# A layer of experts, attention and experts on one core: GpSimd's scatters reordered, one weighing moved to VectorE, and the table of row numbers requested by GpSimd

## The chip, the cores and the metric

One core of a Trainium2 chip runs the whole program in one launch. The metric is the device time of that launch in microseconds (us), the median over runs. Engines are named as the profile names them: PE is TensorE, DVE is VectorE, ACT is ScalarE, POOL is GpSimd, SP is SyncE. SP computes nothing here; it only issues DMA transfers in program order, and a wait in its program holds every transfer behind it.

## What is computed

Input `x` has 8 x 1024 rows of 256 numbers. The layer is a sandwich, cut here to what matters:

```python
def ffn(h):                       # 64 experts, the best 2 per row, 256 places per expert
    x = rmsnorm(h) * rms_w
    probs = softmax(x @ gate_w.T)
    w, ids = top_k(probs, 2); w = w / w.sum()
    buf[e, place] = x[row]        # rows are grouped by expert: this is the scatter
    y = (silu(buf @ w13[:, :I]) * (buf @ w13[:, I:])) @ w2      # per expert
    moe[row] = sum over the 2 chosen experts of w * y[e, place] # and back
    shared = silu(x @ sw_gate) * (x @ sw_up) @ sw_down
    return moe + shared + h

x = x + 0.5 * ffn(layernorm(x))
x = x + attention(layernorm(x))   # three MLPs and a masked, softmax-free attention
x = x + 0.5 * ffn(layernorm(x))   # same weights again: "the second experts"
```

The change is at the passage from the attention to the second `ffn`.

## The kernel before

The attention works on 16 groups of 512 rows, which the code calls halves of a sequence (`HALVES = 16`, `j` or `h` counts them; `last` is 15). While TensorE does the matrix products of group `j`, the other engines finish group `j - 2`: they normalise its rows for the second `ffn`, ask TensorE for the router's logits, choose two experts per row, count how many earlier rows chose the same expert, and so give each row its two slots in DRAM. GpSimd then writes each row to its two slots: `scatter_rows` (L1182) issues 8 indirect DMAs per group into `slot_rows`, 128 rows each. `scatter_meta` (L1197) issues 8 more into `slot_ids`: for each slot the number of the row that sits in it, 4 bytes each.

After the last group nothing of the attention is left to hide this work, so the two last groups (14 and 15) form a chain, here called the passage. For group 15 it runs:

- VectorE `out_statistics` writes `attention_o_under`;
- GpSimd `out_roots` (L1166) takes the power -1/2 (`routing_affine`);
- VectorE `out_scales` (L1521) makes the scale and shift;
- ScalarE `normalise` (L1306) writes the rows, four tiles of 128x256, into `xn_last`, which lies in `attention_t_rows`; each tile raises `normed`;
- `weigh` (L1170) multiplies them by the row `rms_w`, on GpSimd, one instruction for all four tiles;
- TensorE `turn_x` (L1961) transposes them, ScalarE copies them (`attention_w_rows`), TensorE `router` (L1969) makes the logits, VectorE `choose` and `mark` pick the experts, GpSimd `counts` (L1174), TensorE `place_tiles`, VectorE `places` and `slots` give the addresses;
- GpSimd `scatter_rows(15)` issues the 8 row scatters.

GpSimd issues in the order in which its code is written, and between the steps of group 15 it scatters the rows and row numbers of group 14.

The 64 experts follow. SP loads an expert's 256 slots (`load_slots`, L1067, into a ring of `YR` = 4 buffers) and its weights (`load_w13`, `load_w2`, rings of 8; the first eight are loaded long before). Expert `e` goes: TensorE `turn_slots(e)` (L2116), ScalarE and VectorE split the rows and weights in two parts, TensorE `gate_up(e)` (L2129), ScalarE's silu, TensorE `expert_down(e)` (L2139), ScalarE `copy_y(e)` (L1399) into a ring of 4, and GpSimd two indirect DMAs (L1280) that write the 256 results back by row number into `token_rows`. These need the table `who` (`attention_gelu` in the traces), which is `slot_ids` read back. SP loads it: after `load_slots` 0 to 3 its program waits for all row-number scatters, issues the table and only then goes on with `load_slots(4)` and the weights of expert 8. Three waits bind the loop: `load_slots(e)` waits for `turn_slots(e - 4)`; `load_w2(e)` waits for `expert_down(e - 8)`; `copy_y(e)` waits until the scatters of expert `e - 4` have landed.

## Time and profile before

| | us |
|---|---|
| median of 3 runs | 2216.04 |
| lowest and highest of them | 2206.85, 2218.53 |
| the profiled execution | 2217.58 |
| its span, from first to last instruction | 2215.4 |
| share of the span in which PE is busy | 89% |

The profiled execution is the one that the rows come from; it took 2.2 us more than its span and 1.5 us more than the median. Times of rows are us from the start of its span. The passage lies at 1829 to 1874, the experts at 1874 to about 2084, the shared part and the sum behind them.

### The profile page before, as it was taken

The numbers are of one execution on the slowest core, as the hardware profiler recorded it, in microseconds if no ns is written. First come the engines' busy times: TensorE is split into PE (matmuls) and PEld (weight loads), VectorE is DVE, ScalarE is ACT, GpSimd is POOL, SyncE is SP. The second block draws the span as 40 slices with busy tenths as digits, with TensorE's granted clock in tenths as the row PEclk, the third lists the DMA queues.
The fourth block names the chain that finished last, engine by engine and source line by source line (L and its number), as shares of the span: only waits on it lengthen the run. The fifth ranks groups of instructions, "written<-read, shape, count | busy, mean of one in ns | idle before, by whom it ended". The sixth has DMA issues, their size and how long they took to land.

```text
span 2215.4 us, 32427 instructions
## 1 busy us (share of the span) xinstructions
PE 1978.3 (89%) x11044; PEld 1675.5 (76%) x11044; DVE 1324.0 (60%) x3515; ACT 1085.1 (49%) x1988; POOL 1105.9 (50%) x1202
## 2 busy tenths in 40 slices
PE   6886888779999999999999999999999972888887
PEld 4665788658888888888888878878888862887754
DVE  6996555355576566576576575565565442554467
ACT  6774666434454454454454354444453442555643
POOL 5665666453245545545545645645525316555500
PEclk9998999989999999999999999999999985999999
DMA  8433888792032021121121210110100202888778
GB/s 274 144 105 129 269 272 275 245 301 61 1 96 67 30 95 38 59 95 41 56 89 31 73 43 21 52 39 20 58 10 20 86 10 67 274 274 287 240 250 280
DMA packets 236405, 270.06 MB, mean 122 GB/s; under 512 B 25489, under 2 KB 186322, under 8 KB 236242
## 3 DMA queue, kind: packets, MB, share of 16 engines
q1 hardware_dynamic: 199122, 192.40, 27.7%
q0 software_dynamic: 28672, 67.22, 9.3%
q10 hardware_dynamic: 8448, 8.39, 1.1%
q8 instruction: 88, 1.44, 0.3%
q14 instruction: 75, 0.61, 0.1%
HBM read 150.35 MB, written 117.57 MB: 121 GB/s over the span
## 4 chain that ended last, share of the span: by engine, by line
PE 60%; DVE 8%; issue 5%; ACT 4%; POOL 1%; DMA 1%; another core or an unknown queue 1%; SPq 0%; ACTq 0%; DVEq 0%; POOLq 0%
PE attention_ring L1926 20%; PE attention_acc L1956 13%; PE attention_acc L1946 8%; DVE attention_hid_l L1659 2%; PE attention_work L2016 2%; PE attention_work L1999 2%; PE attention_work L2032 2%; PE attention_work L2036 2%; PE attention_acc L2139 2%; PE attention_ring L2129 2%; PE attention_ring L2165 2%; PE attention_acc L2129 1%; PE attention_work L1914 1%; PE attention_ring L2116 1%; PE attention_work L1973 1%
## 5 line engine op out<-in xcount | busy, mean ns | idle before, releaser
L1659 DVE TENSOR_TENSOR attention_hid_l<-attention_gelu,attention_hid_h 128x512 fp32r<-128x512 f32 x384 | 284.5, 741 | 504.4 <-ACT attention_gelu L1303 320.3
L1300 ACT ACTIVATE attention_hid_h<-attention_ring,home_b 128x512 fp32r<-128x512 f32 x384 | 264.2, 688 | 572.6 <-PE attention_ring L1926 500.0
L1303 ACT ACTIVATE attention_gelu<-attention_ring,home_b 128x512 f32<-128x512 f32 x384 | 261.7, 682 | 0.0
L1956 PE MATMUL attention_acc<-attention_hid_h,home_w_h 128*128 128x512 f32 x512 | 203.9, 398 | 21.0 <-DVE home_room L1685 18.7
L1926 PE MATMUL attention_ring<-attention_n_t_h,home_w_h 128*128 128x512 f32 x512 | 206.0, 402 | 1.4 <-DVE attention_n_t_l L1651 1.4
L1926 PE MATMUL attention_ring<-attention_n_t_l,home_w_h 128*128 128x512 f32 x512 | 201.7, 394 | 0.0
L1926 PE MATMUL attention_ring<-attention_n_t_h,home_w_l 128*128 128x512 f32 x512 | 201.6, 394 | 0.0
L1956 PE MATMUL attention_acc<-attention_hid_l,home_w_h 128*128 128x512 f32 x512 | 200.3, 391 | 0.0
L1956 PE MATMUL attention_acc<-attention_hid_h,home_w_l 128*128 128x512 f32 x512 | 200.2, 391 | 0.0
L1147 POOL DMA_INDIRECT home_room<-expert_rows,routing_slots x128 | 135.9, 1061 | 98.3 <-issue 53.8
L648 POOL DMA_INDIRECT experts_xg<-xn_rows,routing_affine x128 | 141.8, 1108 | 71.9 <-PE experts_ps_t L741 35.3
L1280 POOL DMA_INDIRECT token_rows<-home_room,attention_gelu x128 | 127.8, 999 | 97.6 <-ACT home_room L1399 53.0
L1192 POOL DMA_INDIRECT slot_rows<-attention_xn,attention_slot_at x120 | 123.3, 1027 | 95.5 <-DVE attention_meta_at L1595 63.6
L1946 PE MATMUL attention_acc<-home_w_h,attention_hid_h 128*128 128x256 f32 x512 | 145.2, 284 | 0.4 <-issue 0.4
L1203 POOL DMA_INDIRECT slot_ids<-attention_row_id,attention_meta_at x128 | 127.1, 993 | 36.6 <-issue 36.5
L1946 PE MATMUL attention_acc<-home_w_h,attention_hid_l 128*128 128x256 f32 x512 | 144.8, 283 | 0.0
L1946 PE MATMUL attention_acc<-home_w_l,attention_hid_h 128*128 128x256 f32 x512 | 144.5, 282 | 0.0
L1956 PEld LDWEIGHTS attention_acc<-attention_hid_h,home_w_h 128*128 128x128 f32 x512 | 96.9, 189 | 52.2 <-DVE home_room L1685 24.2
L1926 PE MATMUL attention_ring<-attention_m_t_h,home_w_h 128*128 128x512 f32 x256 | 112.3, 439 | 1.4 <-DVE attention_m_t_l L1651 1.4
L1926 PEld LDWEIGHTS attention_ring<-attention_n_t_l,home_w_h 128*128 128x128 f32 x512 | 97.1, 190 | 21.3
L1956 PEld LDWEIGHTS attention_acc<-attention_hid_l,home_w_h 128*128 128x128 f32 x512 | 96.6, 189 | 20.8
L1926 PEld LDWEIGHTS attention_ring<-attention_n_t_h,home_w_h 128*128 128x128 f32 x512 | 97.3, 190 | 19.4 <-DVE attention_n_t_l L1651 1.8
(277 smaller groups left out, 5247.1 us busy)
## 6 DMA issues: line engine op xcount, KB each, us to landing
experts_w<-in_L_ffn_w SPq DMA_DIRECT2D x64, 256.0 KB
expert_rows<-experts_y SPq DMA_DIRECT2D x64, 256.0 KB
slot_rows<-const_zeros SPq DMA_DIRECT2D x16, 1024.0 KB
token_rows<-const_zeros SPq DMA_DIRECT2D x16, 1024.0 KB
home_room<-in_L_ffn_w SPq DMA_DIRECT2D x64, 256.0 KB
home_room<-slot_rows SPq DMA_DIRECT2D x64, 256.0 KB
final_y_rows<-token_rows SPq DMA_DIRECT2D x32, 512.0 KB, 7.4
dispatch_x_in<-in_L_attn_x SPq DMA_DIRECT2D x16, 512.0 KB, 7.1
```

The lines of the kernel that those rows point to most:

```text
L648: pool.indirect_dma_start(out=xg[e % R][:, c, :], out_offset=None, in_=xn_d, in_offset=bass.IndirectOffsetOnAxis(ap=routing["lists"][:, e, ...
L1147: pool.indirect_dma_start(out=ye[:, t, k, :], out_offset=None, in_=y_d, in_offset=bass.IndirectOffsetOnAxis(ap=routing["slots"][:, j * GT ...
L1192: pool.indirect_dma_start(out=xs_d, out_offset=bass.IndirectOffsetOnAxis(ap=slot_at[h % 2][:, k, t:t + 1], axis=0), in_=xn_of(h)[:, t, :], ...
L1203: pool.indirect_dma_start(out=meta_d, out_offset=bass.IndirectOffsetOnAxis(ap=meta_at[h % 2][:, k, t:t + 1], axis=0), in_=row_id[h % 2][:, ...
L1280: pool.indirect_dma_start(out=y2_d, out_offset=bass.IndirectOffsetOnAxis(ap=who[:, e, c:c + 1], axis=0), in_=y[e % YR][:, c, :], in_offset ...
L1300: act.activation(hid[n % PARTS][0][:, :], ring[n % RING][:, :], ACT.Gelu, bias=b1[:, m, c:c + 1])
L1303: act.activation(gelu[n % GELUS][:, :], ring[n % RING][:, :], ACT.Gelu, bias=b1[:, m, c:c + 1]).then_inc(ring_free, 1)
L1659: dve.tensor_tensor(hid[n % PARTS][1][:, :], gelu[n % GELUS][:, :], hid[n % PARTS][0][:, :].bitcast(fp32), ALU.subtract).then_inc(hid_read ...
L1926: last = pe.matmul(ring[n % RING][:, :], w1[m][wp][:, k, c * P:(c + 1) * P], rows_t[xp][:, k, :], start=(q == 0), stop=(q == 2 * len(TERMS ...
L1946: last = pe.matmul(acc[e % 3][:, (t % 2) * D:(t % 2 + 1) * D], hid[s][xp][:, t * P:(t + 1) * P], w2[m][wp][:, c, :], start=(c == 0 and q = ...
L1956: last = pe.matmul(acc[e % 3][:, :], w2[m][wp][:, c, k * P:(k + 1) * P], hid[s][xp][:, :], start=(c == 0 and q == 0), stop=(c == FC - 1 an ...
L2129: last = pe.matmul(ps_gu[e % EF][:, half, :], wt[e % EF][:, k, half * INNER:(half + 1) * INNER], xt[e % EF][:, k, :], start=(n == 0), stop ...
```

## The change

Four edits, all at the passage. (1) GpSimd's `out_roots(15)` comes after 4 instead of 6 of group 14's row scatters; the other 4 follow it, and the row-number scatters of group 14 are split 4, 3 and 1 instead of 5 and 3, the one left over being issued behind the rows of group 15. (2) The weighing of group 15 leaves GpSimd: VectorE does it tile by tile, four instructions, each after the tile's `normed`. A new semaphore `last_weighed` tells of it, and TensorE's `turn_x` and GpSimd's row scatters of group 15 wait for that. VectorE's second split of weights, `split_weights(1)`, now stands behind the weighing. (3) SP no longer waits for the row-number scatters nor loads the table. (4) GpSimd waits for them itself and requests the table, behind its last row-number scatter and ahead of the experts' result scatters.

```diff
@@ sync
             sp.wait_ge(y2_zeroed, 16 * FILLS)
-            for h in (HALVES - 2, HALVES - 1):
-                sp.wait_ge(*scattered(meta_scattered, h))
-            sp.dma_start(who, meta_d[0:SLOTS, :].rearrange("(p e c) a -> p e (c a)", p=P, c=CH)).then_inc(who_loaded, 16)
@@ gpsimd, scatter_rows
                 pool.wait_ge(slots_ready, 4 * (h + 1))
-                pool.wait_ge(weighed, h + 1)
+                if h < HALVES - 1:
+                    pool.wait_ge(weighed, h + 1)
+                else:
+                    pool.wait_ge(last_weighed, GT)
@@ gpsimd
             counts(last - 1)
-            scatter_rows(last - 1, 0, 6)
+            scatter_rows(last - 1, 0, 4)
             out_roots(last)
-            scatter_rows(last - 1, 6, 8)
-            weigh(last)
-            scatter_meta(last - 1, 0, 5)
+            scatter_rows(last - 1, 4, 8)
+            scatter_meta(last - 1, 0, 4)
             counts(last)
-            scatter_meta(last - 1, 5, 8)
+            scatter_meta(last - 1, 4, 7)
             scatter_rows(last)
+            scatter_meta(last - 1, 7, 8)
             scatter_meta(last)
-
+            for h in (last - 1, last):
+                pool.wait_ge(*scattered(meta_scattered, h))
+            pool.dma_start(who, meta_d[0:SLOTS, :].rearrange("(p e c) a -> p e (c a)", p=P, c=CH)).then_inc(who_loaded, 16)
             pool.wait_ge(who_loaded, 16)
@@ vector
             out_scales(last)
             split_weights(0)
+            for t in range(GT):
+                dve.wait_ge(normed, GT * last + t + 1)
+                dve.tensor_tensor(xn_of(last)[:, t, :], xn_of(last)[:, t, :], rms_w[:, :], ALU.mult).then_inc(last_weighed, 1)
             split_weights(1)
@@ tensor, turn_x
-                pe.wait_ge(weighed, j - 1)
+                if j <= HALVES:
+                    pe.wait_ge(weighed, j - 1)
+                else:
+                    pe.wait_ge(last_weighed, GT)
```

On GpSimd, from the row scatters of group 14 to the end of the passage, the order before was as follows (`slot_rows` are row scatters, `slot_ids` row-number scatters; `attention_xn` holds group 14, `attention_t_rows` group 15):

```order
L1192 DMA slot_rows<-attention_xn,attention_slot_at 32768x256 x6
L1168 TENSOR_TENSOR routing_affine<-attention_o_under,const_minus_half 128x2x4
L1192 DMA slot_rows<-attention_xn,attention_slot_at 32768x256 x2
L1172 TENSOR_TENSOR attention_t_rows<-attention_t_rows,routing_rms_w 128x1024
L1203 DMA slot_ids<-attention_row_id,attention_meta_at 32768x1 x5
L1182 TENSOR_TENSOR attention_before<-attention_carry,attention_either 128x64
L1182 TENSOR_TENSOR attention_before<-attention_before,attention_either 128x64 x2
L1182 TENSOR_TENSOR attention_carry<-attention_before,attention_either 128x64
L1203 DMA slot_ids<-attention_row_id,attention_meta_at 32768x1 x3
L1192 DMA slot_rows<-attention_t_rows,attention_slot_at 32768x256 x8
L1203 DMA slot_ids<-attention_row_id,attention_meta_at 32768x1 x8
```

And the same stretch in the changed kernel:

```order
L1193 DMA slot_rows<-attention_xn,attention_slot_at 32768x256 x4
L1166 TENSOR_TENSOR routing_affine<-attention_o_under,const_minus_half 128x2x4
L1193 DMA slot_rows<-attention_xn,attention_slot_at 32768x256 x4
L1204 DMA slot_ids<-attention_row_id,attention_meta_at 32768x1 x4
L1180 TENSOR_TENSOR attention_before<-attention_carry,attention_either 128x64
L1180 TENSOR_TENSOR attention_before<-attention_before,attention_either 128x64 x2
L1180 TENSOR_TENSOR attention_carry<-attention_before,attention_either 128x64
L1204 DMA slot_ids<-attention_row_id,attention_meta_at 32768x1 x3
L1193 DMA slot_rows<-attention_t_rows,attention_slot_at 32768x256 x8
L1204 DMA slot_ids<-attention_row_id,attention_meta_at 32768x1 x9
L1278 DMA attention_gelu<-slot_ids 128x128
```

The roots moved two scatters forward, the weighing (`routing_rms_w`) is gone, one row-number scatter went behind the rows of group 15, and the table's load is new at the end.

On VectorE, at the point where `out_scales(15)` has run, the changed kernel has this (`attention_n_t_l` is the split of an expert's weights; before, its two instructions stood together and the weighing was absent):

```order
L1532 SCALAR_TENSOR_TENSOR routing_affine<-attention_o_mv,routing_affine 128x4
L1808 TENSOR_TENSOR attention_n_t_l<-home_room,attention_n_t_h 128x512
L1848 TENSOR_TENSOR attention_t_rows<-attention_t_rows,routing_rms_w 128x256 x4
L1808 TENSOR_TENSOR attention_n_t_l<-home_room,attention_n_t_h 128x512
L1540 MAX attention_top<-attention_work 128x8 x4
```

The four weighings stand between the two splits, ahead of the search for the best experts.

On SP, before, from the two last stores of the attention's rows on (`home_room<-slot_rows` is an expert's slots, `home_room<-in_L_ffn_w` weights):

```order
L1041 DMA base_rows<-home_room 128x4x256 x2
L1070 DMA home_room<-slot_rows 128x512 x4
L1097 DMA attention_gelu<-slot_ids 128x128
L1070 DMA home_room<-slot_rows 128x512
L1059 DMA home_room<-in_L_ffn_w 128x512
```

And now:

```order
L1042 DMA base_rows<-home_room 128x4x256 x2
L1071 DMA home_room<-slot_rows 128x512 x5
L1060 DMA home_room<-in_L_ffn_w 128x512
```

The table's load no longer stands between the fourth and the fifth expert's slots.

## Rows read from the trace of the kernel before

**Rows 1.** The page's busy time of each engine and its share.

```profile
PE 1978.3 (89%) x11044; PEld 1675.5 (76%) x11044; DVE 1324.0 (60%) x3515; ACT 1085.1 (49%) x1988; POOL 1105.9 (50%) x1202
```

**Rows 2.** Busy time by stretch: stretch, length, engines, PEclk, DMA share, GB/s.

```profile
1829.00:1841.00 12.00, 0.26 (x3) 0.06 (x1) 4.46 (x17) 2.08 (x4) 10.15 (x9) 0.64 0.22 77
...
1890.00:1904.00 14.00, 12.45 (x88) 11.71 (x87) 9.05 (x21) 7.42 (x16) 9.63 (x10) 1.00 0.93 312
1904.00:1910.00 6.00, 5.58 (x41) 5.18 (x40) 3.82 (x7) 4.03 (x9) 2.36 (x3) 1.00 0.64 184
1910.00:2050.00 140.00, 122.16 (x825) 114.20 (x824) 70.02 (x123) 78.64 (x164) 83.52 (x83) 0.96 0.87 282
2050.00:2080.00 30.00, 27.44 (x191) 25.32 (x190) 15.45 (x28) 22.35 (x50) 17.17 (x19) 1.00 0.98 318
```

**Rows 3.** Timeline of GpSimd at the roots and the weighing: start, duration.

```profile
1833.39 0.96 POOL L1192 DMA_INDIRECT slot_rows<-attention_xn,attention_slot_at  x1 [0.30 <-issue]
1834.38 1.68 POOL L1168 TENSOR_TENSOR routing_affine<-attention_o_under,const_minus_half 128x8 f32<-128x8 f32 x1
1836.24 1.04 POOL L1192 DMA_INDIRECT slot_rows<-attention_xn,attention_slot_at  x1 [0.19 <-issue]
1837.58 0.96 POOL L1192 DMA_INDIRECT slot_rows<-attention_xn,attention_slot_at  x1 [0.30 <-issue]
1838.63 2.33 POOL L1172 TENSOR_TENSOR attention_t_rows<-attention_t_rows,routing_rms_w 128x1024 f32<-128x1024 f32 x1
```

**Rows 4.** Timeline of VectorE, ScalarE and TensorE in the same stretch.

```profile
1831.82 0.16 DVE L1519 TENSOR_SCALAR attention_o_under<-attention_o_mv 128x4 f32<-128x4 f32 x1
...
1836.36 1.28 DVE L1805 TENSOR_TENSOR attention_n_t_l<-home_room,attention_n_t_h 128x512 fp32r<-128x512 f32 x2
1836.47 2.08 ACT L1313 ACTIVATE attention_t_rows<-home_room,routing_affine 128x256 f32<-128x256 f32 x4 [9.17 <-DVE routing_affine L1529]
...
1841.02 1.33 PE L1966 MATMUL attention_work<-const_eye,attention_t_rows 128*128 128x128 f32 x5 [11.76 <-POOL attention_t_rows L1172]
```

**Rows 5.** Timeline of VectorE, a product of two 128x256 tiles.

```profile
1882.21 0.42 DVE L1817 TENSOR_TENSOR attention_state<-attention_state,attention_acc 128x256 f32<-128x256 f32 x1
```

**Rows 6.** Timeline of GpSimd from the counts to the first result scatter.

```profile
1850.15 0.30 POOL L1182 TENSOR_TENSOR attention_before<-attention_carry,attention_either 128x64 bf16<-128x64 bf16 x1 [2.96 <-DVE attention_either L1555]
...
1851.76 0.99 POOL L1203 DMA_INDIRECT slot_ids<-attention_row_id,attention_meta_at  x1 [0.15 <-issue]
...
1855.58 0.96 POOL L1192 DMA_INDIRECT slot_rows<-attention_t_rows,attention_slot_at  x1 [0.30 <-DVE attention_meta_at L1595]
...
1864.44 0.96 POOL L1192 DMA_INDIRECT slot_rows<-attention_t_rows,attention_slot_at  x1 [0.31 <-issue]
...
1874.56 0.96 POOL L1203 DMA_INDIRECT slot_ids<-attention_row_id,attention_meta_at  x1 [0.31 <-issue]
1886.74 0.96 POOL L1280 DMA_INDIRECT token_rows<-home_room,attention_gelu  x1 [11.22 <-DMA attention_gelu<-slot_ids]
```

**Rows 7.** Timeline of SP's queue at the end of the passage.

```profile
1866.94 1.76 SPq L1070 DMA_DIRECT2D home_room<-slot_rows  x4
1882.73 0.32 SPq L1097 DMA_DIRECT2D attention_gelu<-slot_ids  x1
1883.10 1.02 SPq L1070 DMA_DIRECT2D home_room<-slot_rows  x1
```

**Rows 8.** Timeline of TensorE, its two waits for slots.

```profile
1873.93 1.96 PE L2116 MATMUL attention_ring<-const_eye,home_room 128*128 128x128 f32 x8 [21.66 <-DMA home_room<-slot_rows]
...
1887.34 0.74 PE L2116 MATMUL attention_ring<-const_eye,home_room 128*128 128x128 f32 x4 [1.95 <-DMA home_room<-slot_rows]
```

**Rows 9.** Timeline of ScalarE, copies of the first and fifth expert's results.

```profile
1884.14 0.59 ACT L1399 ACTIVATE home_room<-attention_acc 128x512 f32<-128x512 f32 x1
...
1897.44 0.59 ACT L1399 ACTIVATE home_room<-attention_acc 128x512 f32<-128x512 f32 x1
```

**Rows 10.** DMA issues, 1850 to 1890: KB, us from issue to landing.

```profile
attention_gelu<-slot_ids SPq DMA_DIRECT2D x1, 64.0 KB, 3.7
```

More of the change, by code:

```diff
@@ L1003, in attention_to_end @@
         odds_ready, f_step, f_scaled, halved = sem("odds_ready", late=True), sem("f_step", late=True), sem("f_scaled", late=True), sem("halved", late=True)
+        last_weighed = sem("last_weighed", late=True)
         f_normed, f_turned, xf_t_ready, sw_weighed = sem("f_normed"), sem("f_turned"), sem("xf_t_ready"), sem("sw_weighed")
```

## The prediction

> **What bounds the kernel now.** The page's busy times come first: TensorE is busy for 89% of the span and no other engine for more than 60% [rows 1]. Over the whole kernel the rule is therefore that only what TensorE waits for counts, and the change touches about 60 us of 2215. So the next view is the table by stretches, then the timeline of each engine through the passage. In 1829 to 1841 TensorE works 0.26 of 12 us [rows 2]: it stands idle for 11.76 us until the weighing on GpSimd is done at 1838.63 + 2.33 = 1840.96 [rows 3, 4]. It works briefly on the logits and is then idle for 21.66 us until the first expert's slots have landed, at 1873.93 [rows 8]. What ends last there is GpSimd's queue and the transfers behind it: the eight row scatters of group 15 start at 1855.58 and the last at 1864.44, SP issues the slot loads at 1866.94, and the first lands 7.0 us later [rows 6, 7, 8]. Behind that, SP stands: its last slot load of four is out at 1868.7, and the next transfer, the table, goes at 1882.73, with the fifth expert's slots at 1883.10 [rows 7]. TensorE waits 1.95 us for these slots, at 1887.34 [rows 8]. From 1910 on the experts run with TensorE busy for 122.16 of 140 us and the DMA engines at 0.87 [rows 2]: neither is full.
>
> **Edit 1, the roots two scatters earlier.** VectorE has their input at 1831.82 + 0.16 = 1831.98, GpSimd starts them at 1834.38, right behind the sixth scatter, which began at 1833.39 [rows 3, 4]. A scatter takes its 0.96 plus 0.30 of issue, 1.27 from start to start: four instead of six end at 1834.35 - 2 x 1.27 = 1831.8, just ahead of the input. From an input to GpSimd's start I take 0.08, the step from ScalarE's last tile (1836.47 + 2.08 = 1838.55) to the weighing at 1838.63 [rows 3, 4]. New start 1832.06, gain 2.32. The chain behind (roots 1.68, VectorE's scales, four tiles on ScalarE) keeps its lengths: tiles done at 1836.23.
>
> **Edit 2, the weighing on VectorE.** On GpSimd it is one instruction that waits for all four tiles and takes 2.33 [rows 3]. On VectorE only the last tile's quarter is left after ScalarE's last tile. The trace of before has no 128x256 product of these two operands; the nearest row is 0.42 for two 128x256 tiles [rows 5], the bounds are 0.42 / 2 (were it to run at twice that rate) and 0.64 (the 128x512 split, 1.28 for two [rows 4]). I take 0.42, plus 0.04 for the hand-over: TensorE can start at 1836.23 + 0.04 + 0.42 + 0.06 = 1836.75 instead of 1841.02. Edits 1 and 2 together gain 4.27, of which edit 2 is 1.95. The first three weighings lie beside ScalarE's tiles (2.08 for four, 0.52 each) and cost nothing. `split_weights(0)` lies ahead of the tiles, `split_weights(1)` behind them; the second is first needed by the second expert, 35 us later. VectorE has nothing else until the logits, so the cover is wide.
>
> GpSimd must not become late in its turn. Roots end at 1833.74, eight scatters (four of rows, four of row numbers) begin at 1833.92 and at 1.27 each, with the 1.34 of the first as in [rows 3], end by 1843.8. The counts may start 4.27 earlier than now, at 1845.9 [rows 6]: 2.0 us of slack. Counts and three row-number scatters, as before, give 1851.3 for the first row scatter of group 15, where it was 1855.58. Before, its addresses and the third row-number scatter were ready within a tenth of a us of each other, so neither hides the gain. The row-number scatter put behind costs only the table 1.27. Slots are then issued by SP at 1866.94 - 4.27 = 1862.7 and expert 0 starts at 1869.7.
>
> A lock between the two engines is a rule that speaks against this edit. The row first: VectorE's two splits ran at 1836.36 for 1.28, beside a row scatter on GpSimd from 1836.24 that took 1.04 instead of 0.96 [rows 3, 4], so 0.08 is all that the pair lost, and the sum stays as it is. The Trainium skill (SBUF — State Buffer, "Who interferes with whom") says that a VectorE instruction with two inputs in SBUF contends with a GpSimd instruction that reads SBUF, and the one that comes second waits for the other's end. Taken by that rule with scatters as readers, the last weighing would begin up to a scatter's length later, and the sum would be about 1 us less; that is the rival "lock" below.
>
> The clock gives nothing back. TensorE is idle for 11.76 us, and the granted clock over 1829 to 1841 is 0.64 [rows 2, 4]: of 12 us some 3.4 at the full 2.4 GHz and the rest at 1.2, so it fell near 1832.4, ahead of 1836.75. The transposes and the router will still run at half clock.
>
> **Edits 3 and 4, the table.** SP may issue the fifth expert's slots when `turn_slots(0)` is done, about 1.0 into the pair at 1873.93, thus at 1875.0 in the old times and 1870.7 in the new; before it was 1883.10, 8.1 later. Loads of slots took 7.0 (1866.94 to 1873.93) and 4.2 (1883.10 to 1887.34) [rows 7, 8]. Even with 7.0 they are there at 1877.7, and TensorE wants them at 1887.34 - 1.95 - 4.27 = 1881.1: the wait of 1.95 goes whole. The loads that SP sent in one burst from 1883 on made DMA engines 0.93 busy in 1890 to 1904, and TensorE was idle for 1.55 there and 0.42 in 1904 to 1910 [rows 2]; spread out, they cost between 0 and 2.0. I take half, 1.0.
>
> The table now goes later by the moved scatter and by GpSimd's own issue. Row numbers: first at 1851.3 + 8 x 1.27 = 1861.4, the ninth begins at 1871.6 and ends at 1872.5. Before, from the last one's end (1874.56 + 0.96 = 1875.52) to SP's issue 7.2 passed; I keep that, since its cause is not in the rows: 1879.7. Landing: SP's took 3.7 [rows 10], and 4.0 to the first result scatter [rows 6, 7]. No row has a plain load issued by GpSimd; its scatters need 0.96 before their bytes go, SP's issue 0.32. Between 3.7 and 7.0 + 1 I take 4.3: result scatters start at 1884.0. The Trainium skill (DMA: Bandwidth & Descriptors, "Specifications") gives about 1 us to the first byte for a DMA that GpSimd issues against about 0.6 for one of SP's; by it the sum for the table would be 0.4 more than SP's, near what I take. Who waits: ScalarE's copy of the fifth result, which needs the first expert's two scatters landed. It stood at 1897.44 [rows 9], now 1897.44 - 7.2 = 1890.2. Two scatters from S are landed at S + 1.27 + 2.5 (the last row scatter of the passage took 2.5 from start to SP's release, 1864.44 to 1866.94). So S may be as late as 1886.4; 1884.0 leaves 2.4. Hidden, but with a thin cover.
>
> **Sum.** 4.27 + 1.95 + 1.0 = 7.2 us. Against the profiled execution's 2217.58 that is 2210.4 (span 2208.2). That execution lies 1.5 above the median, so for the median 2216.04 - 7.2 = 2208.8. All behind expert 5 is a loop of waits among engines and rings, with no fixed date in it, so I let a shift pass through whole.
>
> **Rivals.** In times of the profiled execution; take 1.5 off for the median.
> - Only the head start arrives (chance 0.25). Either the table is later than 1886.4, or the DMA engines bind: 0.87 at 282 GB/s for 140 us and 0.98 at 318 in 2050 to 2080 [rows 2] speak for it; against it speaks that the 0.87 leaves an eighth of their time free. The stage begins 4.27 earlier and keeps just that: 2213.3.
> - More than forecast (0.12). The loads run ahead by all of SP's idle stretch, 7.2 from the last row number to the table, and TensorE's waits in 1910 to 2050 shrink too: 4.27 + 7.2 = 11.5, 2206.1. Against it: the rings are short, and SP is soon back at the pace of `expert_down`.
> - The lock (0.08): 6.2, 2211.4. The 0.08 in the rows is against it; the rule of the Trainium skill above is for it.
> - The change does not act at the roots or the place search (0.05): something else, as the addresses, holds GpSimd; gain 3, 2214.6.
> - Slower (0.05): the table becomes the bound. It used to be loaded while nothing else moved; now slots and weights are in flight. Slots needed 7.0 instead of 4.2 beside the small scatters. If wait and load of the table took twice 11.5, S would be 1872.5 + 23 = 1895.5, and the fifth copy, with the next silu and the next rows' split behind it on ScalarE, and so TensorE, would be 9.1 late: +1.9, 2219.5. It decides from S = 1893.6 on.
>
> The forecast has 0.45.
>
> **How the numbers follow.** About 0.5% (11 us) is what a measurement of this kernel tells from no change. The median forecast is 2208.8. Cases from 11.5 gained to 1.9 lost give medians 2204.5 to 2218; the runs of before alone lie 11.7 apart, so I widen a little to 2201 to 2219. Faster by over 0.5% means under 2205: half of the third case, the edge of the forecast and the runs' scatter give 0.16. Slower by over 0.5% needs 18 us of new waits: 0.03. The rest, 0.81, is within.
>
> **What will show it.** GpSimd's roots at 1832.1; the last of four VectorE weighings ending near 1836.7, each about 0.42; TensorE's transposes after 7.5 idle instead of 11.76; the first row scatter of group 15 at 1851.3; slots issued at 1862.7; the fifth slots issued within 1871 and no wait of TensorE for them; the table issued near 1880 and result scatters from 1884. I would be wrong if the addresses came later than 1851.3, if the fifth copy waited for landed scatters, or if TensorE's idle time in the later experts grew by what the start had saved.

## The result and the profile after

| | us |
|---|---|
| before, median of 20 runs | 2212.78 (2199.78 to 2226.75) |
| changed, median of 20 runs | 2222.46 (2214.09 to 2231.74) |
| ratio, with its 95% interval | 1.0049 [1.0035, 1.0063] |
| changed, profiled execution; its span | 2224.62; 2222.7 |

The change costs 10.8 us by the ratio, 7.7 to 13.9 by its interval; 7.2 saved were forecast. The profiled execution had reached the passage 7.13 us sooner than the one of before, by chance, so below the places are compared by their distance from one instruction, the first row scatter of group 14 on GpSimd: 1826.65 before, 1819.52 after. I call it "offset".

The page's busy line has hardly moved against [rows 1]; only TensorE has 9 us more, with the same number of instructions:

```profile
PE 1987.3 (89%) x11044; PEld 1683.2 (76%) x11044; DVE 1323.8 (60%) x3519; ACT 1085.2 (49%) x1988; POOL 1103.6 (50%) x1202
```

The table by stretches, at the places of [rows 2] moved by 7 us (stretch, length, engines, PEclk, DMA share, GB/s):

```profile
1822.00:1834.00 12.00, 3.82 (x18) 3.29 (x17) 6.05 (x21) 5.05 (x10) 9.44 (x10) 0.68 0.22 77
1883.00:1897.00 14.00, 10.77 (x70) 9.84 (x69) 6.36 (x15) 4.36 (x9) 8.73 (x9) 0.95 0.61 203
1897.00:1903.00 6.00, 3.10 (x13) 3.06 (x14) 1.71 (x3) 1.99 (x4) 2.88 (x3) 0.58 0.42 157
1903.00:2043.00 140.00, 120.56 (x782) 111.74 (x781) 67.50 (x119) 76.03 (x160) 78.11 (x78) 0.92 0.82 269
```

In the first stretch TensorE works 3.82 us where it had 0.26: the head start is there. In the next two it works 13.9 of 20 us where it had 18.0, and in the first of them the DMA engines move 203 GB/s where they moved 312. The granted clock (PEclk) is 0.95, 0.58 and 0.92 in the last three stretches, where it was 1.00, 1.00 and 0.96. The start of the experts is where the gain is lost. From the first copy of an expert's result to the ninth, before and then in the changed kernel:

```profile
1884.14:1912.36 28.22, 24.30 (x168) 22.27 (x166) 15.82 (x33) 15.20 (x33) 15.40 (x16) 1.00 0.87 278
1871.36:1910.25 38.89, 28.51 (x169) 26.05 (x167) 16.16 (x33) 15.55 (x33) 16.06 (x17) 0.82 0.71 191
```

Of the 10.7 us by which this stretch is longer, 6.5 are idle time of TensorE and 4.2 are busy time: nearly the same matmuls at a mean granted clock of 0.82 in place of 1.00.

The timelines of VectorE, ScalarE and TensorE answer to [rows 4]:

```profile
1824.68 0.16 DVE L1522 TENSOR_SCALAR attention_o_under<-attention_o_mv 128x4 f32<-128x4 f32 x1
1827.03 2.08 ACT L1316 ACTIVATE attention_t_rows<-home_room,routing_affine 128x256 f32<-128x256 f32 x4 [6.85 <-DVE routing_affine L1532]
1827.66 1.91 DVE L1848 TENSOR_TENSOR attention_t_rows<-attention_t_rows,routing_rms_w 128x256 f32<-128x256 f32 x4
1829.62 1.97 PE L1975 MATMUL attention_work<-const_eye,attention_t_rows 128*128 128x128 f32 x8 [7.49 <-DVE attention_t_rows L1848]
```

TensorE's transposes stand at offset 10.10, before at 1841.02 - 1826.65 = 14.37: the 4.27 of the forecast to the hundredth, and the idle time of 7.49 too. GpSimd's timeline answers to [rows 3] and [rows 6]:

```profile
1824.93 1.67 POOL L1166 TENSOR_TENSOR routing_affine<-attention_o_under,const_minus_half 128x8 f32<-128x8 f32 x1 [0.23 <-issue]
...
1829.41 0.99 POOL L1193 DMA_INDIRECT slot_rows<-attention_xn,attention_slot_at  x1 [0.31 <-issue]
...
1844.18 0.96 POOL L1193 DMA_INDIRECT slot_rows<-attention_t_rows,attention_slot_at  x1 [0.30 <-DVE attention_meta_at L1598]
...
1864.44 0.96 POOL L1204 DMA_INDIRECT slot_ids<-attention_row_id,attention_meta_at  x1 [0.30 <-issue]
1879.82 0.60 POOL L1278 DMA_DIRECT2D attention_gelu<-slot_ids  x1 [14.42 <-DMA slot_ids<-attention_row_id,attention_meta_at]
1885.70 1.01 POOL L1283 DMA_INDIRECT token_rows<-home_room,attention_gelu  x1 [5.28 <-DMA attention_gelu<-slot_ids]
```

The first row scatter of group 15 is 4.27 earlier too, and expert 0 starts even 5.4 earlier (offset 41.87 against 47.28), since its slots took 5.8 us and not 7.0. But the wait between the last row-number scatter and the table has doubled, 14.42 us in place of 7.2, and the first result scatter starts 5.88 behind the start of the table's issue, where it was 4.01. Result scatters start at offset 66.18, before at 60.09. SP's queue, against [rows 7]:

```profile
1855.56 7.33 SPq L1071 DMA_DIRECT2D home_room<-slot_rows  x5
1862.93 0.44 SPq L1060 DMA_DIRECT2D home_room<-in_L_ffn_w  x1
1869.87 0.33 SPq L1065 DMA_DIRECT2D home_room<-in_L_ffn_w  x1
1870.24 0.43 SPq L1071 DMA_DIRECT2D home_room<-slot_rows  x1
```

SP no longer stands: five slot loads, the weights of expert 8 and the sixth slot load are out while, before, the table was still being waited for. TensorE's waits for slots, against [rows 8], and ScalarE's copies of the fifth and the ninth result, against [rows 9]:

```profile
1861.39 1.95 PE L2125 MATMUL attention_ring<-const_eye,home_room 128*128 128x128 f32 x8 [20.52 <-DMA home_room<-slot_rows]
...
1879.62 1.13 PE L2125 MATMUL attention_ring<-const_eye,home_room 128*128 128x128 f32 x4 [4.25 <-DMA home_room<-slot_rows]
...
1890.59 0.60 ACT L1402 ACTIVATE home_room<-attention_acc 128x512 f32<-128x512 f32 x1 [1.46 <-DMA token_rows<-home_room,attention_gelu]
...
1910.25 0.59 ACT L1402 ACTIVATE home_room<-attention_acc 128x512 f32<-128x512 f32 x1
```

The wait of 1.95 for the fifth expert's slots is gone. The one at 1879.62 is for the sixth's, requested at 1870.24 and 9.4 us on the way. The granted clock falls during this wait and again in a later idle stretch of 5.16 us that ends at 1899.90; behind each, TensorE works for nearly 5 us at half clock:

```profile
1879.60:1884.20 4.60, 4.58 (x19) 4.40 (x20) 1.71 (x3) 1.99 (x4) 0.60 (x1) 0.50 0.77 268
1899.90:1904.70 4.80, 4.80 (x18) 4.33 (x19) 1.42 (x3) 2.01 (x5) 1.82 (x2) 0.50 0.25 87
```

The fifth copy then waits for scatters that have not landed. The ninth copy stands at offset 90.7, before at 85.7. Last, the transfers themselves, in 40 equal slices (busy tenths, GB/s), first the changed kernel from 1861 to 1885:

```profile
DMA  9991502344010135299951499296996459999510
GB/s 397 406 199 15 94 14 17 75 65 31 27 14 27 51 48 75 65 336 366 253 20 7 38 104 41 73 32 85 145 99 58 53 207 353 386 410 418 184 41 0
```

and the kernel before, from 1867 to 1883:

```profile
DMA  0094900041304238999940000000000000040000
GB/s 1 0 77 92 92 0 0 5 113 51 20 26 36 67 51 338 395 390 410 330 132 6 1 1 0 0 0 0 0 0 0 0 0 0 0 20 0 0 0 0
```

Between 1863 and 1880 the changed kernel moves mostly 15 to 100 GB/s, but for a burst near 1872, with engines that often count as busy, though five loads and more are under way. It is back at 400 just as the wait of 14.42 ends. Before, the loads of four experts crept likewise for 5 us and then ran at 330 to 410; after that nothing moved for 6 us, and the table was requested into the quiet.

### The profile page after: what moved, and what is told of

Read it like the earlier page. It is cut to its first block, busy times and chain, and to the rows that moved or that the text cites. A ratio compares the mean times of both kernels' runs of the same rounds, so it can differ in the third digit from the quotient of the medians.

```text
span 2222.7 us, 32431 instructions
## 1 busy us (share of the span) xinstructions
PE 1987.3 (89%) x11044; PEld 1683.2 (76%) x11044; DVE 1323.8 (60%) x3519; ACT 1085.2 (49%) x1988; POOL 1103.6 (50%) x1202
## 4 chain that ended last, share of the span: by engine, by line
PE 59%; DVE 8%; issue 7%; ACT 4%; DMA 1%; another core or an unknown queue 1%; POOL 1%; SPq 0%; ACTq 0%; DVEq 0%; POOLq 0%
PE attention_ring L1932 19%; PE attention_acc L1962 13%; PE attention_acc L1952 7%; DVE attention_hid_l L1662 2%; PE attention_work L2025 2%; PE attention_work L2008 2%; PE attention_work L2041 2%; PE attention_work L2045 2%; PE attention_acc L2148 2%; PE attention_ring L2138 2%; PE attention_ring L2174 2%; PE attention_work L1920 1%; PE attention_acc L2138 1%; DMA home_room<-slot_rows 1%
## 5 line engine op out<-in xcount | busy, mean ns | idle before, releaser
L648 POOL DMA_INDIRECT experts_xg<-xn_rows,routing_affine x128 | 141.9, 1109 | 72.2 <-PE experts_ps_t L741 35.2
```

The source lines that it names most:

```text
L648: pool.indirect_dma_start(out=xg[e % R][:, c, :], out_offset=None, in_=xn_d, in_offset=bass.IndirectOffsetOnAxis(ap=routing["lists"][:, e, ...
```

## The theories

**Contention.** Loads let go while GpSimd's row-number scatters are being written creep, and hold up the completion of the scatters. SP's old wait for the table had kept the two apart. The harm comes from edit 3.

**Late table.** The harm comes from GpSimd requesting the table (edit 4): wait, issue and landing are longer, result scatters queue, copies wait.

**Head start lost.** Edits 1 and 2 themselves give nothing or cost, in a stage of experts that has another bound. This can hold beside either of the others.

The runs fell on four chips beside that of the result (chip A); the kernel before takes 2194.07 on B, 2152.95 on C, 2151.67 on D and 2194.54 on E. Ratios are against it on the same chip. Offsets are of the profiled execution. "Wait" is from the end of the last row-number scatter to the table's issue; in g2 four slot loads go first, and 7.4 is the time to the first of them (9.3 to the table). The kernel before has traces on A and D alone, so on B, C and E offsets are compared across chips; the changed kernel did not run on C and D.

| kernel, chip | ratio, 95% interval | wait | first result scatter | ninth copy |
|---|---|---|---|---|
| before, A | | 7.2 | 60.1 | 85.7 |
| b0 before, D | | 8.7 | 60.2 | 84.0 |
| changed, A | 1.0049 [1.0035, 1.0063] | 14.4 | 66.2 | 90.7 |
| e0 changed, B | 1.0029 [1.0014, 1.0044] | 12.7 | 64.3 | 90.2 |
| e0 changed, E | 1.0032 [1.0017, 1.0047] | 15.5 | 66.8 | 91.5 |
| e1 edits 1 and 2, B | 0.9997 [0.9983, 1.0012] | 7.5 | 56.7 | 81.1 |
| e1 edits 1 and 2, C | 0.9998 [0.9988, 1.0007] | 7.3 | 57.0 | 81.0 |
| e2 edits 3 and 4, B | 1.0023 [1.0008, 1.0037] | 10.2 | 63.4 | 86.9 |
| e2 edits 3 and 4, E | 1.0017 [0.9997, 1.0038] | 8.8 | 61.8 | 85.2 |
| e3 changed, loads held, B | 1.0005 [0.999, 1.0019] | 8.7 | 59.6 | 86.4 |
| f3 one load ahead, C | 0.9992 [0.9981, 1.0003] | 9.2 | 59.2 | 81.4 |
| v2 the same, table by SP, D | 0.9997 [0.9984, 1.0011] | 8.1 | 56.6 | 81.8 |
| f1 no row numbers of group 15, C | 0.9963 [0.995, 0.9976] | 3.5 | 52.8 | 74.6 |
| g2 nothing beside the scatters, E | 1.0053 [1.0036, 1.0069] | 7.4 | 69.1 | 94.5 |

## Experiments: which edit costs

**e1_passage_only.** Edits 1 and 2 alone. Against the changed kernel:

```diff
@@ sync
             sp.wait_ge(y2_zeroed, 16 * FILLS)
+            for h in (HALVES - 2, HALVES - 1):
+                sp.wait_ge(*scattered(meta_scattered, h))
+            sp.dma_start(who, ...).then_inc(who_loaded, 16)
@@ gpsimd
-            for h in (last - 1, last):
-                pool.wait_ge(*scattered(meta_scattered, h))
-            pool.dma_start(who, ...).then_inc(who_loaded, 16)
```

> The first two edits alone: GpSimd's new order with half of the weighing on VectorE; the table of row numbers is loaded by SyncE, ahead of the second experts' slot loads, as before the change. Contention theory (slot loads let go while the row-number scatters are still being written slow those scatters and crawl themselves): SyncE's wait for the table keeps them apart, so the table is requested about 7.2 us behind the last row-number scatter, result scatters begin about 12.8 us behind expert 0's first up product as before, and 4 to 6 us are gained: ratio 0.997 to 0.998. Late-table theory (the harm is that GpSimd issues the table, with a longer wait and landing): the same gain. If instead the first two edits cost time in the later experts, the ratio is 1.00 or above.

Measured: 2191.21 against 2194.07, ratio 0.9997 [0.9983, 1.0012]. The wait and the order of the start came as expected, the gain did not: no difference can be told from zero, and a gain of more than 3.7 us is excluded. Both theories of the table had expected 4 to 6 us; "head start lost" is borne out as far as the time goes.

**e2_table_only.** Edits 3 and 4 alone, in the kernel before: SP's three lines out, GpSimd's three in behind `scatter_meta(last)`.

> The last two edits alone: the table of row numbers is requested by GpSimd behind all counts, and SyncE no longer waits for it; GpSimd's order and the weighing are as before the change. Both theories expect it slower than before: the wait for the table about 14 us in place of 7.2, the fifth expert's slot load 9 us in place of 4 to 7, 9 to 14 us lost, ratio 1.004 to 1.006. If the loss came from the first two edits, it would be 0.998 to 1.001.

Measured: 2197.7, ratio 1.0023 [1.0008, 1.0037]. Slower beyond the interval, though by half of what was expected; the wait was 10.2, not 14.

**e3_hold_loads.** The changed kernel with SP's wait put back, and GpSimd still requesting the table:

```diff
@@ sync
             sp.wait_ge(y2_zeroed, 16 * FILLS)
+            for h in (HALVES - 2, HALVES - 1):
+                sp.wait_ge(*scattered(meta_scattered, h))
```

> The changed kernel with one thing put back: SyncE waits for both halves of the row-number scatters before the slot loads of the fifth expert and those behind it; GpSimd still requests the table. Contention theory: the wait for the table falls from 14.4 to about 7 us, the fifth slot load takes 4 to 7 us, ratio 0.997 to 0.998 as with the first two edits alone. Late-table theory: the table stays late since GpSimd issues it (landing near 5.6 us, results behind it), ratio 1.002 to 1.005.

**e0_after_again.** The changed kernel itself.

> The changed kernel unchanged, on the same chip as the three others, as the measure for them. All theories: ratio near 1.005, and the table waited for about 14 us.

Measured on the one chip: e3 2195.1, ratio 1.0005 [0.999, 1.0019]; the changed kernel 2199.5, ratio 1.0029 [1.0014, 1.0044]. With two lines of waiting no loss against the kernel before can be told. The gain that the contention theory had expected on top (0.997 to 0.998) did not come. GpSimd's timeline in the changed kernel and then in e3:

```profile
1860.53 0.59 POOL L1278 DMA_DIRECT2D attention_gelu<-slot_ids  x1 [12.65 <-DMA slot_ids<-attention_row_id,attention_meta_at]
1866.40 1.00 POOL L1283 DMA_INDIRECT token_rows<-home_room,attention_gelu  x1 [5.28 <-DMA attention_gelu<-slot_ids]
```

```profile
1858.30 0.59 POOL L1280 DMA_DIRECT2D attention_gelu<-slot_ids  x1 [8.72 <-issue]
1863.32 1.00 POOL L1285 DMA_INDIRECT token_rows<-home_room,attention_gelu  x1 [4.43 <-DMA attention_gelu<-slot_ids]
```

The wait falls from 12.65 to 8.72 with the loads held, as contention has it. The late table is left with what e3 has and e1 has not: GpSimd as the one that requests it. That costs the first result scatter 2.9 us (59.6 against 56.7), and 0.0008 in the ratio, less than either interval. The times of chip B alone do not divide the loss: e3's median of 2195.1 lies about halfway between e1's 2191.21 and the changed kernel's 2199.5, and the intervals of neighbours touch. That edit 4 costs little rests on f3 below, which has it too and runs at 0.9992 [0.9981, 1.0003] on chip C. So edit 3 is what costs, shown by the waits and likely by the times; edit 4 costs little if anything.

**e1_again.** Edits 1 and 2 once more.

> The first two edits alone once more, to narrow its interval. If the 4.27 us that the trace shows at expert 0 reach the end, the ratio is 0.998; if the later stretch is paced by transfers that start again only 2.8 us earlier, 0.9985 to 0.9995; if they are lost altogether, 1.000.

Measured on chip C: 2152.3 against 2152.95, ratio 0.9998 [0.9988, 1.0007]. A gain of 0.4 us, at most 2.6: the 4.27 of the passage doesn't reach the end whole. TensorE's wait for the slots of the fifth expert, and the stretch behind it:

```profile
1840.95 1.13 PE L2125 MATMUL attention_ring<-const_eye,home_room 128*128 128x128 f32 x4 [3.23 <-DMA home_room<-slot_rows]
```

```profile
1840.90:1844.10 3.20, 3.15 (x15) 3.15 (x16) 1.29 (x2) 1.60 (x3) 1.65 (x3) 0.50 1.06 395
```

Expert 0 starts some 6 us earlier than in b0 (offset 41.71 against 47.83), but SP issues the fifth slots only 4.4 earlier (53.51 against 57.88). So TensorE's wait for them is 3.23 where b0 has 1.27 and the trace of before on chip A 1.95, and behind it TensorE runs 3.2 us at half clock where b0 stays at 1.00. By the sixth copy 2.9 us of lead are left.

**e0_third, e2_third.** The changed kernel, and edits 3 and 4 alone, on chip E.

> The changed kernel on this chip, to see whether its loss is the same where the experts' stretch is paced by TensorE as much as by transfers. All theories of the passage: table waited for 10 us and more, sixth output copy at 77 to 80 us against 74 to 75 of before, ratio 1.002 to 1.005. If the loss was only of chips with slower transfers, 1.000 or below.

> The last two edits alone on this chip. Contention theory: the slot loads of the first four experts come when the row-number scatters are nearly done (5 us later than in the changed kernel), so the wait is 10 us and not 12 to 14, and the loss about half of the changed kernel's: ratio 1.001 to 1.003, less than e0_third's by 0.001 and more although it lacks the head start of the first two edits.

Measured: 1.0032 [1.0017, 1.0047] and 1.0017 [0.9997, 1.0038], with waits of 15.5 and 8.8. On both chips on which both ran, edits 3 and 4 alone cost less than with the head start of 1 and 2 on top, as contention predicts: the head start brings the loads nearer to the beginning of the row-number scatters. The intervals overlap, on B almost wholly, so the times don't show this order; of the mechanism it is the waits that speak.

## Experiments: what crawls, and what of it is contention

**f1_no_last_ids.** The changed kernel without `scatter_meta(last)`, the eight row-number scatters of group 15; the table waits for group 14's row numbers only. What it leaves out is the return of group 15's results to their rows.

> The changed kernel without the eight row-number scatters of the last group (that part is left out: the results of its tokens go to the spare row); the table waits only for the group before. Contention theory: nothing small is being written when SyncE lets the loads go, so the second experts' first five slot loads and weights 8 come at 200 GB/s and more, the fifth slot load takes 4 to 5 us and not 9, nothing waits for the table, and the time falls by 8 to 14 us against before: ratio 0.994 to 0.997. Late-table theory: the table comes early too, but the loads stay as slow as in the changed kernel (fifth slot load 9 us): ratio 0.997 to 0.999.

Measured: 2144.91 against 2152.95, ratio 0.9963 [0.995, 0.9976]. GpSimd's timeline and SP's:

```profile
1824.37 0.96 POOL L1204 DMA_INDIRECT slot_ids<-attention_row_id,attention_meta_at  x1 [0.30 <-issue]
1828.82 0.59 POOL L1276 DMA_DIRECT2D attention_gelu<-slot_ids  x1 [3.49 <-DMA slot_ids<-attention_row_id,attention_meta_at]
```

```profile
1825.60 7.06 SPq L1071 DMA_DIRECT2D home_room<-slot_rows  x5
1832.71 0.43 SPq L1060 DMA_DIRECT2D home_room<-in_L_ffn_w  x1
```

and the transfers from 1825.6 to 1849.6, slices as above:

```profile
DMA  0698092499944398000000000969849699987999
GB/s 1 72 82 10 0 113 34 157 403 393 410 184 24 130 376 345 0 0 0 0 0 14 0 0 12 234 157 369 314 85 260 109 420 389 324 208 239 381 415 348
```

The same loads are let go at the same place as in the changed kernel. Without the eight small scatters beside them the fifth slot load and expert 8's weights come at 345 to 376 GB/s, TensorE has no second wait for slots, and the ninth copy is at 74.6, where the changed kernel has 90 to 91. The first 4 us of the first four slot loads creep here as well, at 10 to 113 GB/s; the one row-number scatter and the rows that are still being written may be the reason, or the slow start may be the loads' own.

**g2_no_loads_beside.** The other way round, on top of e1: even `load_slots(0)` to `(3)` wait until all row numbers are written, so nothing is loaded beside them.

> The first two edits, with SyncE holding back even the first four slot loads until both halves of the row-number scatters are written, so that nothing at all is transferred beside them; table by SyncE. Contention theory: the wait behind the last row-number scatter falls from 7.3 to 8.7 us to about 3.5 us, as in the kernel without the last group's scatters. If 7 to 8 us are the scatters' own time to completion, it stays there. Expert 0 then starts 7 to 14 us later than in e1, so slower: ratio 1.002 to 1.004.

Measured: 2204.66 against 2194.54, ratio 1.0053 [1.0036, 1.0069]. GpSimd's last row-number scatter and SP's first load:

```profile
1850.86 0.95 POOL L1209 DMA_INDIRECT slot_ids<-attention_row_id,attention_meta_at  x1 [0.30 <-issue]
```

```profile
1859.22 1.76 SPq L1071 DMA_DIRECT2D home_room<-slot_rows  x4
1861.09 0.36 SPq L1100 DMA_DIRECT2D attention_gelu<-slot_ids  x1
```

That is 1859.22 - 1851.81 = 7.4 us with nothing beside. The 3.5 that I expected of the contention theory was wrong: the 7.2 of the kernel before is the scatters' own time, and the first four slot loads don't lengthen it measurably. Behind one such scatter 3.5 us pass (f1), behind nine in a row 7.4. They are issued every 1.27 us; an estimate from the two, if each of the nine takes alike, is 1.27 + (7.4 - 3.5) / 8 = 1.8 us for each to be written, so they pile up. The Trainium skill (DMA: Bandwidth & Descriptors, "Specifications") says that transfers under 512 bytes are done by reading, changing and writing back. These have 4 bytes, and a slow completion would fit; no run here had wider row numbers, so that cause is not shown.

**f3_hold_after_fifth.** The changed kernel with SP's wait behind `load_slots(4)`, one load later than in e3.

```diff
@@ sync
             for e in range(YR, EXPERTS):
                 load_slots(e)
+                if e == YR:
+                    for h in (HALVES - 2, HALVES - 1):
+                        sp.wait_ge(*scattered(meta_scattered, h))
```

> The changed kernel, where SyncE waits for both halves of the row-number scatters one load later than in e3: behind the slot load of the fifth expert, ahead of weights 8. If the crawl comes from the sum of the loads (three more of 128 to 256 KB), one load more is nearly free: wait for the table 8 to 10 us behind the last row-number scatter, ratio as e3, 1.000. If any load beside the row-number scatters delays them, the wait is 12 us and more and the ratio 1.002 to 1.003.

**v2_fifth_then_table.** The same, but SP requests the table, right behind that wait.

> The first two edits; SyncE requests the fifth slot load as soon as its buffer is free, then waits for both halves of the row-number scatters, requests the table itself, ahead of weights 8 and all behind. One load beside the row-number scatters is to cost them at most 2 us (9.20 in f3 against 7.5), the table comes ahead of the loads and lands 1 us sooner than in f3. Contention theory: ratio 0.998 to 0.9995. If the order of table and loads means nothing, the ratio of f3, 0.9992, or above.

Measured: f3 2152.67, ratio 0.9992 [0.9981, 1.0003]; v2 2152.16, ratio 0.9997 [0.9984, 1.0011]. One load beside the scatters is nearly free: waits of 9.2 and 8.1 against 7.2 to 8.7 with the first four slot loads alone. The three or more that the changed kernel lets go make it 12.7 to 15.5. So the size of the overlap matters, not that there is one. f3 falls within its expectation; v2's ratio is the one expected if the order of table and loads means nothing, though its result scatters start 2.7 us sooner. Neither can be told from the kernel before. In both, TensorE now waits for the sixth expert's slots, 3.9 and 4.4 us.

## Experiments: where the head start goes

**f7_weights_early.** On top of e1, `load_w13(8)` and `load_w13(9)` are issued ahead of SP's wait for the last rows and left out of the loop.

> The first two edits alone, as e1, and two loads of weights (w13 of experts 8 and 9, 256 KB each) requested ahead of SyncE's wait for the last rows, where the transfer queues are 0.2 busy, in place of among the second experts' loads. If the stretch of the second experts is paced by its transfers (0.86 busy at 280 GB/s in e1), 0.5 MB less in it is worth 0.5/0.28 = 1.9 us, and e1's own head start adds: ratio 0.997 to 0.999. If the stretch is paced by TensorE, or the early loads delay the row scatters, the ratio is that of e1, 0.9997, or above.

Measured: 2151.84, ratio 0.9998 [0.9987, 1.0008], the ninth copy at 81.8: no gain over e1 (0.9998, 81.0) can be told. The 1.9 us that were expected if transfers pace the stretch lie inside the interval, so this run decides little.

**b0_before_again, f5_less_tensor_work, f6_less_loads**, all on chip D; f5 and f6 are the kernel before with one edit each. f5 leaves out one of three terms of a product and is less exact; f6 leaves out the loads of down weights from the ninth expert on and takes those of the first eight, so its results are not the layer's:

```diff
@@ f5: gate_up of the second experts
-                terms = ((w13_hi, x_hi), (w13_lo, x_hi), (w13_hi, x_lo))
+                terms = ((w13_hi, x_hi), (w13_lo, x_hi))
@@ f6: load_w2; expert_down waits for the first load of its buffer only
                 if e >= WR:
-                    sp.wait_ge(y_ready, e - WR + 1)
+                    return
```

> The kernel before once more, for its trace on this chip. All theories: first output copy 57.5 us behind the first row scatter of group 14, the sixth 73 to 74, table requested 7.2 us behind the last row-number scatter. If TensorE has no waits in the stretch of the experts 6 to 43, it takes 107 us (as e1 on one chip); if it waits for weights, 122 to 129.

> The kernel before, where the second experts' gate and up products leave out one of their three terms (hidden values are less exact): four of some sixteen matmul pieces, 1.2 us of TensorE for each of 64 experts, 77 us in all. If the stretch is paced by its transfers (0.86 to 0.97 busy), the time falls by 0 to 15 us, ratio 0.993 to 1.000; if by TensorE, by 50 us and more, ratio under 0.977.

> The kernel before, where the second experts from the ninth on load no down weights (they use those of the first eight; results differ): 128 of 896 KB for each of 56 experts. If the stretch is paced by its transfers, 0.4 us for each, 25 us in all, ratio 0.988; where TensorE has no waits in it, at most 5 us, ratio 0.998 to 1.000.

Measured: f5 2139.17 against 2151.67, ratio 0.9944 [0.9927, 0.996]; f6 2141.7, ratio 0.9946 [0.9931, 0.9961]. The stretch from the 6th to the 44th copy, in b0, f5 and f6 (length, PE, PEld, DVE, ACT, POOL, PEclk, DMA share, GB/s):

```profile
1858.20:1966.80 108.60, 107.25 (x771) 101.94 (x771) 64.96 (x116) 71.51 (x153) 73.37 (x77) 1.00 0.95 321
```

```profile
1857.06:1958.66 101.60, 92.42 (x618) 82.75 (x619) 66.04 (x118) 71.58 (x154) 74.22 (x77) 1.00 1.00 347
```

```profile
1861.69:1968.19 106.50, 106.41 (x770) 102.67 (x771) 65.20 (x117) 71.39 (x153) 73.65 (x77) 1.00 0.89 285
```

On this chip both are all but full: with less work TensorE has waits and the DMA engines stand at 1.00; with fewer bytes TensorE is busy for 106.41 of 106.50. Either cut gains only some 0.5%, 12.5 and 10 us by the medians; for f6 that is neither of the two expectations (0.988, or 0.998 to 1.000). The same stretch of the profile before, on chip A, took 129.2 us:

```profile
1900.40:2029.60 129.20, 113.56 (x774) 106.21 (x775) 65.99 (x117) 72.66 (x154) 77.46 (x77) 0.97 0.86 275
```

There TensorE is idle for 15.6 us, nearly all of it waiting for split weights, and nothing is full. The stage's pace differs by 20% between chips A and D, and on A, B and E it has 119 to 129 us from one profiled execution to the next. That is far more than 4.27, and one trace of it proves nothing about a gain of that size. From the last copy to the end every profile has 117.5 to 117.8 us.

## Why the prediction was wrong

**Edits 1 and 2 at the passage: right.** Roots, weighings, TensorE's start and the row scatters of group 15 moved as worked out (4.27), and four weighings took 1.91 together, 0.5 each, hidden behind ScalarE's tiles but for the last. The rival "lock" is refuted: scatters beside the weighings took 0.99 and 0.96.

**"I keep that, since its cause is not in the rows": this step failed.** The 7.2 from the last row number to the table was carried over to a kernel in which other loads run beside it; it measured 14.4, 12.7 and 15.5 in three traces. The rows had held a warning that I used only for the rival: slot loads took 7.0 us beside the scatters and 4.2 without. e3 shows the step alone: hold the loads and the wait is 8.7, on the chip on which the changed kernel has 12.7.

**"The wait of 1.95 goes whole", "spread out, they cost between 0 and 2.0": wrong in effect.** The fifth expert's wait went, and came back as 4.25 for the sixth. The loads were not spread out; they crept beside the scatters and delayed each other. The result scatters were to start 4.3 after the start of the table's issue and started 5.9 after it; the larger part of their lateness is that of the issue, offset 60.3 where 53.1 was forecast.

**"The clock gives nothing back": right at the passage, but the sum has no term for it behind.** TensorE's two longest idle stretches at the start of the experts, 4.25 and 5.16 us, were followed by work at half clock. From the first to the ninth copy this makes 4.2 of 10.7 us, a cost that the forecast put at nothing.

**The threshold was right, its price was not.** Result scatters were not to be later than offset 59.7 (1886.4 in times of before), and in the changed kernel they come at 66.2, against 57.3 forecast. The fifth copy does wait, 1.46, as in the rival "slower", which put its own threshold at 66.9. That rival, at 0.05, has the right mechanism, table and loads in each other's way; but it priced one late copy, +1.9, and nothing for TensorE's wait for the sixth slots or for the clock. The ninth copy is 5 us late in the trace and the end 10.8 by the runs of chip A, 6.4 and 7.0 on B and E. In the trace of chip A the copies stay 5 late up to the 44th, and further 9.6 us come between the 44th and the last (77.9 where it was 68.3):

```profile
2027.23:2105.16 77.93, 64.97 (x397) 58.05 (x396) 30.75 (x55) 41.37 (x90) 39.91 (x42) 0.89 0.74 249
```

Other traces on A, B and E have 68 to 74 there, e1's 72.2 among them, so how much of this the change causes and how much is scatter isn't shown. That the result scatters issued back to back behind the late table, with copies waiting for them, are what holds the start up is argued from 1885.70 on, not shown either. What ScalarE waited for in the 6 us ahead of 1897.93 the rows don't tell.

**"I let a shift pass through whole": not borne out.** e1 has the fifth copy 1.2 to 2.9 and the ninth 3.0 to 4.6 us earlier, compared across chips, and ends 0.4 to 0.7 earlier by the ratios. Part of the head start goes at once: SP resumes behind the last row-number scatter, and that one is only 3.1 us earlier (45.8 against 48.9), since nine of them now stand behind the rows in place of eight. Part goes in the longer wait for the fifth slots, which are held behind the same scatters, and in the half clock after it. Of what is left at the ninth copy I can say that at most 2.6 us arrive; where the rest is lost stays open, as single traces of the stretch differ by more. f1 on chip C, whose ninth copy is 9.4 us earlier than in b0 on chip D, does carry 8.0 to the end, so a large shift does pass.

No version that does the whole work beats the kernel before beyond the interval; f3 (0.9992) comes nearest.

## What to carry to other kernels

A wait that looks idle in one queue may be the fence that keeps two kinds of traffic apart: before a load is let go earlier, look up what is being written at that time, and compare rows of the same load in and out of its company. A head start counts only up to the next thing that hangs on another chain; follow the last instruction of the queue that the next stage waits for, here the row numbers and not the rows. A wait of TensorE can cost more than its length: look at the granted clock behind it, and at busy time that grew with the same instructions. A shift of a few us doesn't pass through a long stage as a matter of course; measure it by runs, not by one trace.

## What was not expected of the hardware

- Eight or nine indirect scatters of 128 times 4 bytes, issued every 1.27 us, were complete 7.2 to 8.7 us behind the last one's end, also with nothing beside (7.4); a single one took 3.5 (f1).
- Beside them, loads of 128 to 256 KB moved mostly at 15 to 100 GB/s with DMA engines counted as up to 0.9 busy, and at 350 to 420 GB/s as soon as they were written. With three or more such loads let go beside them the scatters' completion took 12.7 to 15.5 us, with loads from the last scatter's end on 8.8 and 10.2 (e2), with one load 8.1 and 9.2.
- GpSimd issued a plain load in 0.60 us where SP takes 0.32. It landed in 3.9 to 5.6 us, and in 2.2 to 3.7 when SP issued it ahead of the other loads.
- TensorE's granted clock was 0.50 over 1879.6 to 1884.2 and 1899.9 to 1904.7, behind waits of 4.25 and 5.16 us, and over 3.2 us behind a wait of 3.23 in e1; behind the waits of 1.27 (b0) and 1.95 (before) at the same place it stayed at 1.00.
- The same kernel took about 2152 us on two chips and 2194 to 2213 on three. Of the 66 us between the traces of A and D, 43 lie ahead of the passage and 21 in the second experts from the 6th to the 44th copy, which moved 275 GB/s on A and 321 on D.
